# A gate and router part in another order on all engines, with two buffers for gated rows and reloaded results

## What is computed

```
h = tok_attention(x)                                  # embedding, attention, norm
h = h + attn(layernorm(h))                            # recurrent attention:
    out = scan(state * (1 - b k k) + b v k) . q       #   32 sequences, 16 heads
    out = layernorm(out) * ln_g + ln_b
    out = out * silu(x @ Wg);  return out @ Wout
h = h + ffn(layernorm(h))                             # routed experts:
    probs  = softmax over tokens of (x @ gate_w.T + gate_b)   # 32 experts
    vals, idx = top 8 tokens of each expert
    merged = sum of the 8 tokens, weighted by vals
    o = gelu([merged, 1] @ w1) ; o = [o, 1] @ w2      # w1, w2: 32 experts
    out[token] += o * vals
```

## Time and profile before

| | us |
|---|---|
| median of 3 runs | 963.61 |
| lowest and highest | 963.23, 966.36 |
| profiled execution | 960.83 |
| its span in the trace | 958.7 |
| TensorE busy | 720.2 (75%) |
| VectorE busy | 650.3 (68%) |
| ScalarE busy | 309.9 (32%) |
| GpSimd busy | 422.4 (44%) |

### The profile page before, as it was taken

How to read it: one execution, slowest core, us unless ns; L and a number is a source line. 1 busy time by engine, 2 the same in 40 slices (tenths; PEclk the granted TensorE clock), 3 DMA queues, 4 the chain that set the end, 5 groups by cost and what they waited for, 6 DMA issues and landing times. The chain is left out here.

```text
span 958.7 us, 20788 instructions
## 1 busy us (share of the span) xinstructions
PE 720.2 (75%) x7932; PEld 484.6 (51%) x7932; DVE 650.3 (68%) x898; ACT 309.9 (32%) x498; POOL 422.4 (44%) x225
## 2 busy tenths in 40 slices
PE   2566659794888898888888888866877759866743
PEld 2344434343666667667666666644555523322221
DVE  2699956776999999999999999953555421001004
ACT  2443423442334333443343343323444321110100
POOL 1443200000899999999999999951111000000000
PEclk9799869996999999999999999977999959887765
DMA  4000010000001000000000000007510079999946
GB/s 101 1 0 0 0 46 0 0 0 13 7 12 35 13 10 9 9 11 11 11 11 11 11 11 12 13 15 245 198 44 23 1 293 399 406 414 419 408 167 211
DMA packets 48889, 86.32 MB, mean 90 GB/s; under 512 B 5232, under 2 KB 32432, under 8 KB 48848
## 3 DMA queue, kind: packets, MB, share of 16 engines
q1 hardware_dynamic: 43248, 81.23, 23.0%
q10 hardware_dynamic: 5600, 4.53, 1.5%
HBM read 76.31 MB, written 9.44 MB: 89 GB/s over the span
## 5 line engine op out<-in xcount | busy, mean ns | idle before, releaser
L789 POOL TENSOR_TENSOR read<-state,q_pos 128x1024 f32<-128x1024 f32 x128 | 301.4, 2358 | 43.7 <-DVE state L884 34.6
L884 DVE TENSOR_TENSOR_SCAN state<-fac,ps_up 128x1024 f32<-128x1024 f32 x128 | 291.6, 2281 | 12.3 <-ACT fac L833 12.3
L833 ACT ACTIVATE fac<-ps_xf 128x1016 f32<-128x1016 f32 x128 | 130.2, 1017 | 232.1 <-PE ps_xf L914 232.1
L914 PE MATMUL ps_up<-hot,utab 64*128 64x128 f32 x2048 | 149.0, 285 | 37.5 <-DVE state L884 35.1
L914 PEld LDWEIGHTS ps_up<-hot,utab 64*128 64x128 f32 x2048 | 127.0, 189 | 88.1 <-DVE state L884 49.5
L914 PE MATMUL ps_xf<-hot,xtab 64*128 64x128 f32 x2048 | 139.2, 275 | 0.0
L914 PEld LDWEIGHTS ps_xf<-hot,xtab 64*128 64x128 f32 x2048 | 127.4, 189 | 0.7
L798 POOL TENSOR_TENSOR utab<-tab 128x1024 f32 (+1 forms) x32 | 64.6, 2020 | 119.3 <-SPq L85 119.3
L955 PE MATMUL ps_o<-read,sel 128*32 128x256 f32 x1024 | 82.0, 393 | 4.2 <-POOL read L789 4.2
L875 DVE TENSOR_TENSOR xtab<-tab,ps_k 128x1024 f32<-128x1024 f32 x64 | 76.5, 1196 | 1.5 <-PE ps_k L906 1.5
L382 POOL TENSOR_TENSOR logit<-score,logc 128x1024 f32<-128x1024 f32 x16 | 37.6, 2353 | 68.1 <-ACT prob L433 44.7
(11 more groups left out here) (198 smaller groups left out, 923.8 us busy)
## 6 DMA issues: line engine op xcount, KB each, us to landing
w_sb<-in_L_ffn_w SPq DMA_DIRECT2D x32, 2048.0 KB, 19.5
rec_out<-osb SPq DMA_DIRECT2D x128, 32.0 KB, 1.5
ao<-rec_out SPq DMA_DIRECT2D x8, 512.0 KB, 4.0
out_dram<-res ACTq DMA_DIRECT2D x8, 512.0 KB, 2.8
tok<-in_x SPq DMA_DIRECT2D x2, 512.0 KB, 8.2
exp_out<-eo SPq DMA_DIRECT2D x8, 128.0 KB
oq<-exp_out SPq DMA_DIRECT2D x2, 512.0 KB, 4.6
w_nat<-in_L_tok_Wq SPq DMA_DIRECT2D x1, 256.0 KB, 9.7
```

Of the source, the lines that this page charges most:

```text
L789: nc.gpsimd.tensor_tensor(read[n % 2][:], state[n % 4][:].rearrange("p (b i t) -> p b i t", b=2, i=IB), q_pos[x.s][:, :, x.k].unsqueeze(2) ...
L833: nc.scalar.activation(fac[n % 2][:].rearrange("p (n t) -> p n t", t=T)[:, :, 1:], ps_x[:].rearrange("p (n t) -> p n t", t=T)[:, :, 1:], A ...
L884: nc.vector.tensor_tensor_scan(state[n % 4][:], fac[n % 2][:], ps_u[n % 2][:], 0.0, ALU.mult, ALU.add)\
L914: last = nc.tensor.matmul(dst[:, b * 512 + col * T:b * 512 + (col + 1) * T], stationary[rows], pos[rows], start=True, stop=True)
```

## The change

- `each_step` runs t from -3 to 6 in the first block and from 7 to 9 in the tail (before: -1 to 7 and 8 to 9). Each engine's `work(t, live)` calls the same pieces in another order and for other quads: in step t TensorE now does x2 of quad t - 1, the merge of t - 2, the gates of t + 1, the logits of t - 1, the first half of the projection of t + 1, z of t + 2, the reloaded results of t + 3, the picks of t - 1 and the second half of the projection.
- `ao` and `y_t` get two buffers each, and the reload's semaphore is split in two. The waits of `scale_rows`, `transpose_x2` and `transpose_z` are set for the new order.
- Quads 0 and 1 are reloaded by SP within the recurrence, each after the stores of its turn have landed (before: quad 0 alone). The last four stores of the recurrence move into the first block of the part (`m["last_store"]`).
- The router weights are transposed into `ps_l` instead of `ps_z`; TensorE waits for their copy before the first logits only. `gw` moves to the space of the tables.

The diff, with unchanged lines left out where a piece of code stays as it was:

```diff
@@ -91,15 +91,15 @@
...
-        for name, shape in (("w_out", [P, KT, E]), ("ln_gb", [P, 2, KT]), ("gw", [X, E]), ("gb", [P, 1])):
+        for name, shape in (("w_out", [P, KT, E]), ("ln_gb", [P, 2, KT]), ("gb", [P, 1])):
...
-        m["ao"] = sb(tables, "ao", [P, QB, KT, T], side="right")
+        m["ao"] = [sb(tables, f"ao{i}", [P, QB, KT, T], side="right") for i in range(2)]
...
-        for name, shape in (("cnt", [P, PAIRS]), ("stats6", [P, PAIRS, 6]), ("same_half", [P, P])):
+        for name, shape in (("cnt", [P, PAIRS]), ("stats6", [P, PAIRS, 6]), ("same_half", [P, P]), ("gw", [X, E])):
@@ -753,7 +753,7 @@
...
-        o_w, o_ld = sem("o_w"), sem("o_ld")
+        o_w, o_ld = sem("o_w"), [sem(f"o_ld{i}") for i in range(2)]
@@ -769,14 +769,18 @@
...
-            for w in range(4):
-                store(0, w)
-            for k in range(KT):
-                sp.wait_ge(o_st[k], START + 64 * 2)
-            load_quad(sp, m, 0)
-            with nc.sync.Fori(1, TURNS) as i:
+            for q in range(2):
+                for w in range(4):
+                    store(q, w)
+                for k in range(KT):
+                    sp.wait_ge(o_st[k], START + 64 * 2 * (q + 1))
+                load_quad(sp, m, q)
+            with nc.sync.Fori(2, TURNS - 1) as i:
...
+            for w in range(3):
+                store(TURNS - 1, w)
+            m["last_store"] = lambda: store(TURNS - 1, 3)
@@ -1001,8 +1005,8 @@
 def load_quad(eng, m, i):
-    eng.dma_start(m["ao"][:].rearrange("p j k t -> p (j k) t"),
-                  m["rec_out"][QB * i:QB * (i + 1)].rearrange("b (k p) t -> p (b k) t", p=P)).then_inc(m["o_ld"], 16)
+    eng.dma_start(m["ao"][i % 2][:].rearrange("p j k t -> p (j k) t"),
+                  m["rec_out"][QB * i:QB * (i + 1)].rearrange("b (k p) t -> p (b k) t", p=P)).then_inc(m["o_ld"][i % 2], 16)
@@ -1019,7 +1023,7 @@
...
-    y_t = sb("y_t", [P, 2, KT, 2, T])
+    y_t = [sb(f"y_t{i}", [P, 2, KT, 2, T]) for i in range(2)]
@@ -1051,7 +1055,7 @@
         def each_step(tail, work):
-            for t in range(QUADS, QUADS + 2) if tail else range(-1, QUADS):
+            for t in range(QUADS - 1, QUADS + 2) if tail else range(-3, QUADS - 1):
...
         def sync_program(sp, tail):
@@ -1062,22 +1066,23 @@
                 for h in range(2):
                     load_w2(sp, a, QB, h, m["w2_sb"][1], w2_ld[1])
...
+            m["last_store"]()
             for k in range(KT):
...
             def load(q):
-                sp.wait_ge(o_at, START + q)
+                sp.wait_ge(o_at, START + q - 1)
                 load_quad(sp, m, q)
-            load(1)
             load(2)
+            load(3)
             load_bias(sp, a, m, wbias)
             for h in range(2):
                 load_w1(sp, a, 0, h, m["w1_sb"][0], w1_ld[0])
-            load(3)
+            load(4)
             for h in range(2):
                 load_w2(sp, a, 0, h, m["w2_sb"][0], w2_ld[0])
-            for q in range(4, QUADS):
+            for q in range(5, QUADS):
                 load(q)
         def gpsimd_program(pool, tail):
@@ -1092,10 +1097,10 @@
...
             def work(t, live):
-                if live(t + 1):
-                    first_root(t + 1)
                 if live(t):
                     second_root(t)
+                if live(t + 3):
+                    first_root(t + 3)
@@ -1140,34 +1145,35 @@
             def scale_rows(q):
...
-                act.wait_ge(o_h, START + q)
+                act.wait_ge(o_h, START + max(q - 1, 0))
...
-                    last = nc.scalar.activation(y_t[:, :, k].rearrange("p s q t -> p s (q t)"),
+                    last = nc.scalar.activation(y_t[q % 2][:, :, k].rearrange("p s q t -> p s (q t)"),
...
             def work(t, live):
-                if live(t - 2):
-                    copy_picks(t - 2)
-                    copy_sums(t - 2)
+                if live(t):
+                    copy_h2(t)
                 if live(t - 1):
                     copy_x2(t - 1)
                 if live(t - 2):
+                    copy_sums(t - 2)
+                if live(t + 2):
+                    normalise(t + 2)
+                if live(t - 2):
                     copy_merged(t - 2)
-                if live(t + 1):
-                    normalise(t + 1)
                 if live(t - 1):
                     exponential(t - 1)
-                if live(t):
-                    copy_h2(t)
-                if live(t + 1):
-                    scale_rows(t + 1)
+                if live(t + 2):
+                    scale_rows(t + 2)
+                if live(t - 1):
+                    copy_picks(t - 1)
...
-                nc.scalar.copy(gw_t[:], ps_z[:, 0, 0, 0:KT * X].rearrange("p (k x) -> p k x", k=KT)).then_inc(o_gwt_ok, 1)
+                nc.scalar.copy(gw_t[:], ps_l[:, 0:KT * X].rearrange("p (k x) -> p k x", k=KT)).then_inc(o_gwt_ok, 1)
@@ -1204,7 +1210,7 @@
             def gate(q):
...
-                y = y_t[:].rearrange("p s k q t -> p s (k q t)")
+                y = y_t[q % 2][:].rearrange("p s k q t -> p s (k q t)")
@@ -1227,17 +1233,18 @@
...
             def work(t, live):
-                if live(t - 1):
-                    normalise_h2(t - 1)
                 if live(t + 1):
-                    input_statistics(t + 1)
+                    gate(t + 1)
                 if live(t - 1):
                     softmax_input(t - 1)
+                if live(t):
+                    h2_statistics(t)
+                if live(t - 1):
                     pick(t - 1)
                 if live(t):
-                    h2_statistics(t)
-                if live(t + 1):
-                    gate(t + 1)
+                    normalise_h2(t)
+                if live(t + 3):
+                    input_statistics(t + 3)
@@ -1245,11 +1252,11 @@
...
             def transpose_in(q):
-                pe.wait_ge(o_ld, START + 16 * q + 16)
+                pe.wait_ge(o_ld[q % 2], START + 16 * (q // 2) + 16)
...
-                        last = nc.tensor.transpose(ps_a[:, j, k * P:(k + 1) * P], ao[:, j, k], ident[:])
+                        last = nc.tensor.transpose(ps_a[:, j, k * P:(k + 1) * P], ao[q % 2][:, j, k], ident[:])
@@ -1268,7 +1275,7 @@
             def transpose_x2(q):
...
-                pe.wait_ge(o_ev, START + min(q + 2, QUADS))
+                pe.wait_ge(o_ev, START + min(q + 3, QUADS))
@@ -1281,7 +1288,7 @@
...
-                        nc.tensor.matmul(ps_h[:, s, cols], y_t[:, s, k, half], w_out[:, k], start=k == 0, stop=False)
+                        nc.tensor.matmul(ps_h[:, s, cols], y_t[q % 2][:, s, k, half], w_out[:, k], start=k == 0, stop=False)
@@ -1312,7 +1319,7 @@
             def transpose_z(q):
...
-                pe.wait_ge(o_xtok, START + max(q - 1, 0))
+                pe.wait_ge(o_xtok, START + max(q - 2, 0))
@@ -1324,32 +1331,34 @@
...
             def work(t, live):
-                if live(t + 1):
-                    transpose_in(t + 1)
-                if live(t - 2):
-                    merge(t - 2)
                 if live(t - 1):
                     transpose_x2(t - 1)
                 if live(t - 2):
-                    transpose_sums(t - 2)
-                if live(t):
-                    project(t, 0)
-                if live(t - 1):
-                    logits(t - 1)
-                if live(t):
-                    project(t, 1)
+                    merge(t - 2)
                 if live(t + 1):
                     gates(t + 1)
-                    transpose_z(t + 1)
+                if live(t - 1):
+                    if t == 1:
+                        pe.wait_ge(o_gwt_ok, START + 1)
+                    logits(t - 1)
+                if live(t - 2):
+                    transpose_sums(t - 2)
+                if live(t + 1):
+                    project(t + 1, 0)
+                if live(t + 2):
+                    transpose_z(t + 2)
+                if live(t + 3):
+                    transpose_in(t + 3)
                 if live(t - 1):
                     transpose_picks(t - 1)
+                if live(t + 1):
+                    project(t + 1, 1)
...
-                    last = nc.tensor.transpose(ps_z[:, 0, 0, k * X:(k + 1) * X], gw[:, k * P:(k + 1) * P], ident[0:X, 0:X])
+                    last = nc.tensor.transpose(ps_l[:, k * X:(k + 1) * X], gw[:, k * P:(k + 1) * P], ident[0:X, 0:X])
...
-                pe.wait_ge(o_gwt_ok, START + 1)
```

## The result

The change makes the kernel faster by more than was forecast: 933.11 us (median of 4 runs, 931.73 to 934.13) against 963.42 us for the kernel before beside it, ratio 0.9679 with a 95% interval of 0.9655 to 0.9704. The forecast was 943.5 us in a range of 937 to 954. The profiled execution took 932.7 us, its span is 930.6 us.

What follows compares the result with a forecast made beforehand. The gate and router part was taken as bound by a chain between engines, the experts by their weights. Terms +1.5 - 21.1 - 9.1 + 8.6 = -20.1 gave 940.7 profiled, plus 2.8 for the median: 943.5 us, range 937 to 954.

Steps and rivals of the forecast that it cites:

- the experts' stretch: First reuse of weight space to the end of the span: forecast unchanged at 166.06 us.
- the six steps: Gates of quad 1 to gates of quad 7: 11.2 us a step, 67.2 instead of 88.28, -21.1 us.
- the tail: Second block to last merged rows: a step longer, 20.8 us instead of 12.2, giving back 8.6 us.
- the end follows the merged rows: Kernel's end moves one for one with the weight issue at 792.64, which stands 8.84 us behind the last merged rows.
- the weights had 6 to 8 us to spare: Second set of weights: land at about 765, next issue at 772.5, so DMA idles 7 to 8 us.
- the picks cost nothing: Rival, each step keeps a hand-over: a late exponential delays the picks, 1 to 2 us a step, median 952; chance 0.07.
- reloads came in time: Rival, late reload: quads 4 and 5 queue behind weights, TensorE waits once or twice for 3 to 8 us, 949; chance 0.06.
- the gain arrived: Rival, nothing arrives at the end: the gain vanishes into the experts' waits, within 0.3%; chance 0.03.
- Start: Part's first block to gates of quad 1: forecast 25.7 us; the start loses 1.5 us net, the earlier block start included.
- Last quad: Gates of quad 7 to the second block: 10.2 us instead of 19.26, -9.1 us.
- hand-over: Recurrence's last copy to the part's first block: 0.5 us instead of 2.42; without four store issues it begins 1.9 us sooner.
- the rival of 995 us: Rival, the clock drops: six steps at the lower clock take 19.8 us each, 51.6 us more in all; chance 0.04.

Runs made afterwards that it cites:

- wait_picks6: Changed kernel, with SP waiting in the second block for the picks of quad 6 before issuing the second set of weights: 932.61 us.
- late_tail: Changed kernel in its new order, with the second block beginning one step later (t = 8 and 9 in the tail): 934.26 us.

## Why the prediction was wrong, and where it was right

**What failed is the size of the sum's terms.** The forecast gained 20.1 us and the median moved by 30.3. The miss, 943.5 - 933.11 = 10.4 us, has three parts. The terms of the part and the experts took 6.84 us less than their forecast (292.46 against 299.3); the largest are the experts' stretch, put at no change (2.1), the six steps (1.5) and the tail (1.4). The code ahead of the first mark ended 1.13 us sooner (638.14 against 639.27), less than it varies by in one kernel. And I added 2.8 us for the distance of the median from the profiled execution; it was 0.4, so 2.4 us of the miss are that term. By the later series of the changed kernel, 936.48, the miss would be 7.0: a third of it hangs on when it was measured.

**The mechanism was right.** TensorE is the bound of the new step, x2's wait and the copy's are gone, the clock holds, the end follows the merged rows with 8.84 us between (8.84 measured), and the weights had 6 to 8 us to spare. None of the rivals decided: in the steady steps the picks cost nothing (in the step shown the exponential ended at 710.50 and VectorE wanted it at 711.80), reloads came in time with two buffers, the gain arrived.

**Term by term all sizes were off to one side.** The sum moved by 292.46 - 319.43 = -27.0 (-25.8 by the two second profiles), and was to move by -20.1:
- *Start* (forecast 25.7 from block to gates, measured 24.70, and 23.05 without the spell): from the first projection to the next gates 9.64 us passed instead of 10.4. The first half of the projection took 4.19 where I had the old 4.65, since its first half microsecond ran at full clock, and the transposes 1.81 instead of 2.0. The trend I gave, that the start is dearer than before, holds (+2.36), but it was to lose 1.5 net, and with the hand-over it lost 0.2.
- *Six steps* (67.2 against 65.68): I charged six full steps. The first has no merge, logits, sums or picks yet, though it waits 1.39 us for the gating (10.54), and the last has no reloaded results (10.85). In the four others (11.07) the wait for the gating was 0.38 instead of 0.55 where the sums stand ahead of it, and 0.82 in the one without them.
- *Tail* (20.8 against 19.44): I took transposes and logits of quad 6 from the old tail's rows at the lower clock. They ran at the higher one, 1.07 and 0.64 us instead of 1.97 and 1.08, which is 1.3 of the 1.4 us.
- *Last quad* (10.2 against 9.60) and *hand-over* (0.5 against 0.28): rounded up. The items of the last quad as I listed them add up to 10.06, and the picks were with TensorE 6.6 us behind the gates instead of 7.0.
- *Experts* (no change forecast, 163.92 against 166.06): this stretch was 164.56 in the second profile of the kernel before, and 162.63 to 164.92 in all others but one, whose weights were held back until the merged rows were complete. So most of these 2 us is spread of that stretch, which the two kernels show alike, and not the change. That the full queue at the first reuse causes it was a theory of mine; with as little time left for the weights as before (20.77 us, wait_picks6) it was 164.56, within what the others show, so it explains little. Where the spread comes from stays open.

What failed beside the sizes is the range. Its lower end, 937, allowed a gain of 26.6, while the bounds of the terms stood at a start 2.5 better and steps of 10.6: 6 x 0.6 + 2.5 = 6.1, which all but used it up, with nothing for the tail or for the spread of stretches that the change doesn't touch.

**The clock.** Stretches of the changed kernel, columns as in the earlier trace rows:

```profile
646.50:650.10 3.60, 3.60 (x18) 3.27 (x18) 0.00 (x0) 1.45 (x2) 0.00 (x0) 0.50 0.09 26
650.60:654.00 3.40, 1.41 (x18) 1.18 (x15) 2.76 (x11) 0.29 (x1) 1.21 (x2) 1.00 0.79 202
654.00:657.40 3.40, 3.40 (x11) 2.16 (x9) 0.00 (x0) 1.64 (x4) 0.00 (x0) 0.51 0.95 305
657.40:746.20 88.80, 76.55 (x635) 56.10 (x631) 58.96 (x239) 44.47 (x86) 15.29 (x20) 1.00 0.37 135
```

The granted clock was 1.00 (2.4 GHz) for 88.8 us on end in the new steps. Before that it rose at 650.6 behind 3.6 us of nothing but transposes and half a microsecond of gates, fell to half (1.2 GHz) at 654.0, half a microsecond behind TensorE's 2.0 us wait for the gating, and rose again. In the variants without that spell the same place reads (late_tail):

```profile
653.33 1.98 PE L1316 MATMUL pq_h<-onehot,g_tab 64*128 64x128 f32 x16
...
656.73 1.99 PE L1291 MATMUL pq_h<-w_out,y_t 128*128 128x256 f32 x8 [1.42 <-DVE y_t L1214]
```

There the clock rose a microsecond later (13.3 us behind the block's start instead of 12.2), the gates ran at half clock and the wait was 1.42 us, and the clock held. Between the start of these gates and the first projection 3.40 us passed in both. The kernels differ in this stretch by the clock alone, so the spell makes the 1.65 us between 24.70 and 23.05. Why the clock fell behind the one wait and not behind the other stays open. The Trainium skill (TensorE: Matmul & The Clock Gate, Part 4: PE-mode transpose) says that transposes do not count as activity like matmuls; as far as it was to speak against this change, the trace does not bear it out. The clock held through sixteen transposes in a row in each step, with matmuls on both sides of them, and the rival of 995 us did not come.

## What to carry to other kernels

When a hand-made pipeline is bound by a chain of hand-overs, give each engine first what the bound engine wants next and last what is wanted a step later, and look for the buffer that makes that order possible: here one 4 KB-a-partition buffer carried 12 of the 27 us, 3 of them by the clock. Where a stage ends in a load that needs its space and in a result that feeds the next stage, find which of the two is late before moving either; the other's slack can be measured by holding it back, as sharply as the stretches behind it repeat. And of a forecast's terms, take each from the row at the clock that the new order will have, and charge the first and last steps of a pipeline with only the work that they hold. Profile the kernel before twice: 2 us of this miss were in a stretch that differed by 1.5 us between two profiles of the same kernel.

## What was not expected of the hardware

Moving four DMA issues out of a block's end was worth 2.14 us by itself and 4.2 up to the gates of quad 1, since the same start then spent less time at half clock (until 13.0 us instead of 18.3). A kernel's start can so gain or lose 1.7 to 2.1 us by edits that add no work there, even by edits to later code only, and the same kernel repeats it: 24.70 and 24.63, 22.34 and 22.37. By contrast the code ahead of the part ended at 638.14 and at 642.18 us in two profiles of the same kernel.
